# Transposing half of the first batch's rows from a copy in a single-pass format

## The reference

```python
xn = _layernorm(x, axis=-1)
x = x + _L0_attn_ref(xn, ...) + _L0_ffn_ref(xn, ...)

# in _L0_attn_ref: 16 heads of 128, with a rotary part of 64; latent widths 64 (kv) and 192 (q)
kv_c = x @ W_kvd + b_kvd
q_c = x @ W_qd + b_qd
scores = jnp.einsum('bhqd,bhkd->bhqk', q, k) * scale      # q, k: an unrotated and a rotated part
probs = jax.nn.softmax(jnp.where(causal, -1e9, scores), axis=-1)
ctx = jnp.einsum('bhqk,bhkd->bhqd', probs, values)
return ctx @ W_o + b_o
# in _L0_ffn_ref: one product with a weight whose rows are made +-alpha
```

## Time and profile before

| what | value |
|---|---|
| median of 3 runs | 1452.0 us (1451.02 to 1452.54) |
| profiled execution | span 1452.4 us from the first to the last instruction; the page gives no other time for it |
| PE busy | 1405.6 us, 97% of the span |
| ACT, DVE, POOL busy | 1203.6 us (83%), 1155.3 us (80%), 992.0 us (68%) |
| mean granted TensorE clock | 0.989 of full speed |
| DMA | 111.27 MB, 77 GB/s on average |

### The profile page before, as it was taken

How to read it: one execution, slowest core, us unless ns; L and a number is a source line. 1 busy time by engine, 2 the same in 40 slices (tenths; PEclk the granted TensorE clock), 3 DMA queues, 4 the chain that set the end, 5 groups by cost and what they waited for, 6 DMA issues and landing times.

```text
span 1452.4 us, 27576 instructions
## 1 busy us (share of the span) xinstructions
PE 1405.6 (97%) x9826; PEld 1278.5 (88%) x9826; DVE 1155.3 (80%) x2756; ACT 1203.6 (83%) x2553; POOL 992.0 (68%) x571
## 2 busy tenths in 40 slices
PE   6789999999999999999999999999999999999997
PEld 4679999998899999998898999998889999999987
DVE  5568898876778888887677888888677888888887
ACT  4458889997788888898687888899777988888886
POOL 5667767867667667768665777777765776666750
PEclk9899999999999999999999999999999999999998
DMA  7952322121323322211233222221232322221100
GB/s 221 304 165 58 92 63 60 51 63 49 87 66 102 91 63 63 63 33 46 77 91 81 61 86 63 63 59 52 62 74 75 94 62 63 63 63 48 37 23 30
DMA packets 39997, 111.27 MB, mean 77 GB/s; under 512 B 7685, under 2 KB 16182, under 8 KB 39862
## 3 DMA queue, kind: packets, MB, share of 16 engines
q1 hardware_dynamic: 35152, 92.69, 23.6%
q0 software_dynamic: 4544, 16.78, 3.4%
q10 hardware_dynamic: 166, 0.03, 0.0%
HBM read 49.71 MB, written 13.63 MB: 44 GB/s over the span
## 4 chain that ended last, share of the span: by engine, by line
PE 83%; ACT 6%; POOL 3%; DVE 3%; DMA 3%; issue 1%; SPq 1%; POOLq 0%; DVEq 0%; ACTq 0%
PE turn L1472 16%; PE ring L1417 11%; PE u_ps L1490 8%; PE ring L1449 8%; PE ring L1447 8%; PE u_ps L1491 8%; PE ring L1448 8%; PE o_ps L1510 4%; PE o_ps L1511 4%; PE ring L1430 2%; ACT probs L737 2%; PE ring L1362 1%; PE ring L1356 1%; POOL k_rope L321 1%; DVE probs L1006 1%; DMA wv_scratch<-wv_parts 1%
## 5 line engine op out<-in xcount | busy, mean ns | idle before, releaser
L1006 DVE TENSOR_SCALAR_CACHE_REDUCE probs<-ring,c_t 128x1024 f32<-128x1024 f32 (+7 forms) x512 | 413.6, 809 | 106.1 <-PE ring L1449 101.2
L1016 DVE TENSOR_TENSOR probs_lo<-turn,probs_hi 128x512 fp32r<-128x512 f32 (+1 forms) x640 | 401.0, 630 | 69.2 <-ACT probs_hi L746 64.4
L746 ACT ACTIVATE probs_hi<-turn 128x512 fp32r<-128x512 f32 (+1 forms) x640 | 350.7, 550 | 115.0 <-PE turn L1472 109.0
L737 ACT ACTIVATE probs<-probs,row_min 128x1024 f32<-128x1024 f32 (+7 forms) x512 | 394.3, 771 | 11.7 <-DVE probs L1006 9.1
L1472 PE MATMUL turn<-ident,probs 128*128 128x128 f32 x2304 | 386.6, 275 | 6.0 <-ACT probs L737 3.7
L1490 PE MATMUL u_ps<-probs_hi,kv_nat 128*128 128x256 f32 x1152 | 315.2, 303 | 0.0
L1472 PEld LDWEIGHTS turn<-ident,probs 128*128 128x128 f32 x2304 | 286.5, 141 | 31.8 <-ACT probs L737 9.3
L1491 PE MATMUL u_ps<-probs_lo,kv_nat 128*128 128x256 f32 x1152 | 290.7, 282 | 0.0
L1447 PE MATMUL ring<-k_hi,q_hi 128*128 128x512 f32 (+2 forms) x768 | 280.0, 365 | 0.0
L1449 PE MATMUL ring<-k_hi,q_lo 128*128 128x512 f32 (+2 forms) x768 | 263.9, 344 | 0.0
L1448 PE MATMUL ring<-k_lo,q_hi 128*128 128x512 f32 (+2 forms) x768 | 263.1, 343 | 0.0
(11 more groups left out here) (229 smaller groups left out, 2590.6 us busy)
## 6 DMA issues: line engine op xcount, KB each, us to landing
wp<-wp_scratch SPq DMA_DIRECT2D x31, 640.0 KB, 4.1
swapped<-k_rope SPq DMA_DIRECT2D x128, 128.0 KB, 2.3
wv<-wv_scratch SPq DMA_DIRECT2D x31, 512.0 KB, 3.3
swapped<-q_y SPq DMA_DIRECT2D x62, 128.0 KB, 2.3
swapped<-q_x SPq DMA_DIRECT2D x62, 128.0 KB, 2.3
wp_scratch<-wp_parts POOLq DMA_DIRECT2D x7, 640.0 KB, 5.6
k_hi<-qb_kv_hi SPq DMA_DIRECT2D x16, 256.0 KB, 3.7
k_lo<-qb_kv_lo SPq DMA_DIRECT2D x16, 256.0 KB, 5.0
```

Of the source, the lines that this page charges most:

```text
L737: act.activation(p, p, ACT.Exp, scale=-1.0, bias=row_min[:, r:r + 1], accum_out=row_sum[:, g % 4, w, h:h + 1]).then_inc(exp_ready, 1)
L746: act.activation(probs_hi[:, r % 4, 0:width], turn[r % 2][:, 0:width], ACT.Identity).then_inc(turned_hi, 1)
L1006: dve.tensor_scalar(probs_of(g, w, h), ring[slot_of(entry)][:, KEY_COLUMN[qt]:KEY_COLUMN[qt] + keys], c_t[b % 2][:, qt, ds(pair * 2 + h, 1 ...
L1016: dve.tensor_tensor(probs_lo[:, r % 4, 0:width], turn[r % 2][:, 0:width], probs_hi[:, r % 4, 0:width].bitcast(F32), ALU.subtract).then_inc ...
```

## The change

For batch 0, tiles 0 to 3, PE no longer transposes from `xn`. DVE still writes these rows to `xn`, but now signals a new semaphore `rows_ready`. SP, between its last weight load and `stack(0)`, waits for that and issues one transfer inside SBUF: 128 partitions by 4 tiles by 256 features of fp32 (512 KB) from `xn` to `xn_words`, which is the memory of `kv_stack` (not yet used then), declared F32R. PE waits for ACT's half (`xn0_ready` of 1) and for the transfer (`words_loaded`), and transposes tiles 0 to 3 in F32R from the copy, with an identity that is F32R memory too, and tiles 4 to 7 as before. Other batches and all other transposes are as before; the identity's memory is the same 128x128 words under two types.

```diff
-        ident, ident_bf, mask_bf = sb("ident", [P, P]), ...
+        ident_words, ident_bf, mask_bf = sb("ident_words", [P, P], F32R), ...
+        ident = ident_words[:, :].bitcast(F32)
...
+        xn_words = kv_stack[:, :].rearrange("p (t n) -> p t n", n=HID)
...
+            def load_words():
+
+                sp.wait_ge(rows_ready, 1)
+                sp.dma_start(xn_words.bitcast(F32), xn[:, 0:NT // 2, :]).then_inc(words_loaded, 16)
...
             load_heads(1)
+            load_words()
             stack(0)
...
-            pool.affine_select(out=ident[:, :], in_=ident[:, :], ...
+            pool.affine_select(out=ident_words[:, :], in_=ident[:, :], ...
...
                 for t in range(NT // 2):
                     last = dve.tensor_scalar(xn[:, t, :], x_sb[:, t, :], ...)
-                last.then_inc(xn0_ready, 1)
+                last.then_inc(rows_ready, 1)
...
                     if k == 0 and b == 0:
-                        pe.wait_ge(xn0_ready, 2)
+                        pe.wait_ge(xn0_ready, 1)
+                        pe.wait_ge(words_loaded, 16)
...
                     for t in range(NT):
-                        mm = pe.transpose(to[:, t * P:(t + 1) * P], xn[:, t, k * P:(k + 1) * P], ident[:, :])
+                        features = slice(k * P, (k + 1) * P)
+                        if b == 0 and t < NT // 2:
+                            mm = pe.transpose(to[:, t * P:(t + 1) * P].bitcast(F32R), xn_words[:, t, features], ident_words[:, :])
+                        else:
+                            mm = pe.transpose(to[:, t * P:(t + 1) * P], xn[:, t, features], ident[:, :])
```

More of the change, by code:

```diff
@@ L132, in sem @@
             return ctx.enter_context(nc.semaphore(name))
-        ident, ident_bf, mask_bf = sb("ident", [P, P]), sb("ident_bf", [P, P], BF16), sb("mask_bf", [P, P], BF16)
+        ident_words, ident_bf, mask_bf = sb("ident_words", [P, P], F32R), sb("ident_bf", [P, P], BF16), sb("mask_bf", [P, P], BF16)
+        ident = ident_words[:, :].bitcast(F32)
         cos, sin = sb("cos", [P, SEQ]), sb("sin", [P, SEQ])
@@ L208, in build @@
         cols_full, cols_ready = sem("cols_full"), sem("cols_ready")
-        norm_step, norm_log, norm_inverse, xn0_ready = sem("norm_step"), sem("norm_log"), sem("norm_inverse"), sem("xn0_ready")
+        norm_step, norm_log, norm_inverse, rows_ready, xn0_ready = (
+            sem(n) for n in ("norm_step", "norm_log", "norm_inverse", "rows_ready", "xn0_ready"))
         head_turned, turned_w_ready, fold_full, fold_hi, fold_lo = (
@@ L220, in build @@
         xn_ready, residual_ready = sem("xn_ready"), sem("residual_ready")
+        words_loaded = sem("words_loaded")
         xnt_ready, down_ready, down_hi, down_lo = sem("xnt_ready"), sem("down_ready"), sem("down_hi"), sem("down_lo")
@@ L578, in _ @@
             pool.wait_ge(ident_made, 1)
-            pool.affine_select(out=ident[:, :], in_=ident[:, :], compare_op=ALU.not_equal, fill=1.0, base=0,
+            pool.affine_select(out=ident_words[:, :], in_=ident[:, :], compare_op=ALU.not_equal, fill=1.0, base=0,
                                pattern=[[-1, P]], channel_multiplier=1).then_inc(ident_made, 1)
```

## The result

The changed kernel takes 1454.8 us (median of 18 runs) where the kernel before, beside it, takes 1453.0 (18 runs). The ratio of runs made side by side is 1.0018, with an interval of 1.0010 to 1.0027: 2.6 us slower, 1.5 to 3.9 (the two medians alone differ by 1.8). The forecast was +3.5 with a range of -1.0 to +6.5 around the time before, so time and direction are inside it. The prediction called slower what lies over 1454.9, with a chance of 0.51; the median falls just short of that, yet the interval excludes that nothing changed. The path by which the 2.6 us arise is only in part the one that was forecast.

What follows compares the result with a forecast made beforehand. From about 90 us PE bounds the kernel; before, a chain of `kr`, POOL's issues and the third pair's store sets the start. That store, 3.5 us later, adds +3.5 to the median 1452.0: 1455.5, range 1451.0 to 1458.5.

Steps and rivals of the forecast that it cites:

- The cheaper transposes: PE's F32R transposes of batch 0, tiles 0 to 3: 0.6 us saved, worth nothing by itself before 5.60 us of idle PE.
- The copy's landing: SP's copy before PE's transposes: lands 8.3 us after issue, at 26.3, so PE stands 4.0 us; bounds 21.3 and 29.1.
- the rival with an early copy: At PE's wait: the copy lands in time, nothing behind it moves; +0 to +1 us, 1452.0 to 1453.0; chance 0.22.
- the one at 29 us or later: Rival: copy waits behind POOL's backlog, PE stands 6.8 us; +5.5 to +7.5 us, 1457.5 to 1459.5; chance 0.15.
- PE's clock after the stand: PE after waiting for the copy: lower granted clock, extra loss 1.7 us, within 0 to 2.9.
- forecast for `stack(0)`: SP's first stacking issue after the down product moves by 3.8 us, from 34.76 to 38.6.
- What the copy takes from `kr`: POOL's `kr` load on the start chain: the copy takes engine time from it, 2.0 us later, bounds 0 to 2.3.
- The store that ends the chain lands when those bytes are through: Full DMA stretch from 36 to 64 us: starts with `stack(0)`, so the third pair's store lands 3.5 us later.
- The rest of PE's delay falls into the gaps: PE's lateness beyond `stack(0)` is absorbed by the idle gaps of 5.60 us on PE and 10.21 us on ACT.
- The clock that stays up: Rival: PE's gap before 66.22 shortens, clock stays 2.4 GHz, 3 us come back; 1452.5, or 1449.5 with in-time copy; chance 0.18.
- the sum: Whole kernel: +3.5 us, the third pair's store's delay carried one for one to the end, giving 1455.5; forecast case chance 0.45.
- the prediction's own signs: One SP issue at 18.0; PE idle 3 to 5 us; `kr`, `stack(0)`, third pair's store and projection (about 92.5) all later.

Runs made afterwards that it cites:

- e3: Changed kernel without the transfer: DVE writes tiles 0 to 3 straight into the F32R tile, rounding them; ratio 1.0006 to the kernel before (0.9996 to 1.0016).
- e2: Kernel before, no copy; PE waits ahead of the transposes for a bias load landing about when the copy does; ratio 1.0027 (1.0012 to 1.0042).
- e4: Changed kernel with DVE doing head 8's and 9's low parts ahead of the bias and last rotation; ratio 1.0010 to the kernel before (0.9999 to 1.0020).
- e1: Kernel before plus the copy, unused: PE transposes from `xn` as before, only SP waits, ahead of `stack(0)`; ratio 1.0003 (0.9994 to 1.0013).
- e12: Kernel before plus two unused 512 KB copies, the second into `qb_stack`'s memory, PE waiting for neither; ratio 1.0010 (1.0000 to 1.0020).
- e5: Changed kernel with `turn_head(4)`, `fold(2)` and `fold(3)` ahead of the transposes on PE, ACT and DVE; ratio 1.0015 to the kernel before (1.0006 to 1.0024).
- e6: Kernel before, no copy, with `turn_head(4)`, `fold(2)` and `fold(3)` ahead of the transposes on PE, ACT and DVE; ratio 1.0011 (1.0002 to 1.0020).
- e9: Changed kernel with key rotations behind low parts of heads 8, 9 and bias on DVE, ACT's keys behind `folded_high(11)`; ratio 1.0047 to the kernel before.
- e11: Kernel before, no copy, with transposes ahead of `fold(0)` and the first down product ahead of `fold(1)`; ratio 1.0007 (0.9997 to 1.0017).
- e8: Changed kernel with POOL waiting for the copy ahead of its `wo` and following loads; ratio 1.0031 to the kernel before (1.0020 to 1.0042).
- e10: Kernel before, no copy, with key rotations behind low parts of heads 8, 9 and bias on DVE, ACT's keys behind `folded_high(11)`; ratio 1.0014.

## Why the prediction was right, and which of its steps failed

**The cheaper transposes: right.** Forecast 0.6 us, worth nothing by itself. 0.35 was saved in the changed kernel (3.08 to 2.73) and 0.12 in e3, which shows no gain.

**The copy's landing: right, a little short.** Forecast 8.3 us and a stand of 4.0; measured 9.5 and 5.12, and 9.1 to 10.8 over the runs with a first copy of any size. That the row taken from the earlier trace rows, copies of a quarter of the bytes, came so near is in part luck: the forecast had the copy share the engines from its issue on, and the trace has 6 us without a packet and then 3 us of them. The copy landed at 26.2, so neither the rival with an early copy nor the one at 29 us or later came about, though a copy that first waits while POOL's queue has the engines is what the latter supposed.

**PE's clock after the stand: oversized.** Forecast 1.7 us. The first down product behind the stand took 3.60 us, as before. PE's lateness was 5.3 at the transposes; at ACT's copy of the latents it was 35.06 - 16.65 - (31.04 - 17.99) = 5.4. So PE lost some 0.4 there (5.4 less 5.3, plus the 0.35 saved), all of it between the transposes and the down product, where `turn_head(4)` ran at the slow pace (0.42 us for the first of its products at 29.05, against 0.27 at 25.42). And it wasn't a lower granted clock: after the stand of 5.12 us that stayed at 1.00, in each window from 22 to 34.

```profile
28.00:30.00 2.00, 2.00 (x15) 1.00 1.04 408
```

What slowed PE there isn't shown. The term also took 1.2 of 2.9 us as lost in the time before, where its own figures, 0.20 less 0.11 over sixteen transposes, give 1.4. The short landing and the large clock term offset one another: forecast lateness 5.1, measured 5.4; forecast for `stack(0)` 3.8, measured 4.1.

**What the copy takes from `kr`: failed.** Forecast 2.0 us on POOL's chain. POOL was ready for `qr` no later in the changed kernel (22.64), and `kr` landed 7.2 to 8.9 us after issue in the kernels with a copy and 7.8 to 8.6 in those without. The step rested on near equal shares between the queues; in this stretch q1 had no packet until `kr` was nearly through. The Trainium skill ("DMA: Bandwidth & Descriptors", section "Queues, rings and completion order") says that each engine goes round the queues it has work for and drains one packet before it turns to the next. The trace agrees once q1 moves, with 106 of 209 packets on q1 from 23 to 25 us; from 18 to 22, where 236 packets of q0 and none of q1 moved, either the engines did not take turns or the copy's work had not reached them, and no run here tells which.

**"The store that ends the chain lands when those bytes are through": failed, and with it the third pair's store 3.5 us later.** The step took `stack(0)` for the first issue of the stretch and so its start. It is not: POOL issues `load_heads(2)` at 34.54, ahead of `stack(0)` at 37.52, and the store is seen 0.9 us *earlier* after the rows than before (45.1 against 46.0). That it did not move is read from one trace; in e2 and e4 the store was 3.0 and 2.2 us late.

**"The rest of PE's delay falls into the gaps": failed for the keys.** True for the folds of heads 2 to 7, false for the first projection, which the prediction didn't follow any further. It comes 6.4 us later after the rows, and the swap that needs it falls among POOL's stores: 9.0 us to landing instead of 3.7. In the trace of the changed kernel this is the term that took the store's place.

**The clock that stays up: refuted.** The gap on PE ahead of `turn_head(8)` did not vanish (4.53 us against 4.75), and the granted clock was at 0.50 in the changed kernel too, in each one-us window from 65 to 74. PE then stood again, 2.32 us for head 8's low part, and the lower level lasted longer than before instead of going away. That is where the 0.6 us at the first products of the FFN come from.

**So the sum** of +3.5 against +2.6 was near for a reason that was half right, and the nearness is in part luck: the +3.5 was the delay of a store that did not move in the trace, and the way that the trace does show was priced at nothing. Shown: late transposes suffice for a loss of this size without any copy (e2); the bytes alone, without PE waiting for them, cost little or nothing (e1, e12); the loss stays when PE does other work in the wait (e5). e6 is slower than before, by 0.3 to 2.9 us, with late latents and neither a copy nor idle PE, but in a new order of folds. Seen in the trace, but not isolated by a run: the last link, from late latents over the swap and DVE's stand to the first block. e4 and e9 attacked it by order and left it open, e2 and e4 have the store late beside it, and e11 has the same stands at a smaller loss, if any. So that link stays open. Among the kernels, a projection of pair 1 that comes later after the rows goes with a larger ratio on the whole (e3 at 70.3, e1 at 72.2, after at 73.2, e9 at 77.1), with e6, e8 and e10 cheaper than their places; but that sets one execution beside a median, and e12 shows that one execution can be 1.9 us off.

Of the prediction's own signs, SP's one new issue, the stand ended by the copy and the place of `stack(0)` came (38.9, counted from the rows of the kernel before). `kr` did not move, ACT passed the store at 63.1 on that count instead of 66.5 to 68, and the projection of pair 1 came at 91.3 instead of 92.5.

No version here beats the kernel before.

## What to carry to other kernels

A copy that makes the input of a cheaper instruction is to be priced by its landing in its own stretch. Here, beside the other queue's backlog, two thirds of that were a wait ahead of the first packet, and halving the bytes, at the same number of packets, did not help. When a step is late, follow its product to each consumer, down to the small transfer that is issued behind it: in the trace of this change 5 us on PE did little harm in PE's own gaps, and showed up where swaps of 128 KB slid from ahead of a burst of stores into it. Before an end is taken to move with the first issue of a stretch, see which issue is first.

## What the runs showed of the hardware that was not expected

A copy inside SBUF on SP's queue got no packet from 18 to 22 us while POOL's queue had all sixteen engines, although it was issued at 16.68; 256 KB landed after 9.4 us and 512 KB after 9.1 to 10.8, against 3.3 for 512 KB with a quiet queue. Both sizes were 144 packets.

The granted clock of TensorE stayed at 1.00 over a stand of 5.12 us in the changed kernel (windows from 22 to 34 us), and was at 0.50 after stands of 5.60 and 4.75 us in the kernel before (and 0.50 in each window from 67 to 72).

Two executions of nearly the same kernel can differ by more than a microsecond at a batch boundary, with the granted clock as the difference that shows. Where nothing was changed, windows of the kernel before and of the changed one, between the same two loads of `wp` (issued at 749.03 and 800.44 before, at 750.26 and 800.09 after):

```profile
749.00:801.00 52.00, 50.98 (x365) 47.03 (x365) 39.93 (x94) 41.72 (x91) 31.70 (x14) 0.97 0.33 87
```

```profile
750.00:801.00 51.00, 50.06 (x371) 46.20 (x370) 40.49 (x98) 42.43 (x92) 32.24 (x14) 1.00 0.35 91
```

51.41 us at a granted clock of 0.97 against 49.83 at 1.00; at the next boundary 49.26 (1094.78 to 1144.04) against 47.78 (1094.40 to 1142.18), again at 0.97 and 1.00. These 3.1 us are more than the 2.6 looked for, and turn the comparison of two spans around.
